# Turning a 128x32 block of row maxima: one TensorE transpose and a copy, or four 32x32 transposes on VectorE

## The chip, the cores and the metric

One core of one Trainium2 chip runs the whole kernel. The metric is the device time of one execution in microseconds. Before the change three runs took 1509.4, 1510.23 and 1512.35 us (median 1510.23).

## The reference

Eight batches of 512 tokens with 128 features go through three blocks: a layer of attention and a mixture of eight experts, an attention layer with rotary positions and shared keys, and the first block again with the same weights. All attention is over the 512 tokens of a batch. Cut to what matters here, it is

```
scores = einsum('bhqd,bhkd->bhqk', q, k) * scale
attn = softmax(scores, axis=-1)
out = einsum('bhqk,bhkd->bhqd', attn, v)
```

with 16 heads of 8 features, and the first and the last block end in

```
one_hot = one_hot(argmax(logits, axis=-1), E)
h = gelu(einsum('td,edh->teh', xf, w1)); y = einsum('teh,ehd->ted', h, w2)
out = einsum('te,ted->td', one_hot, y)
```

The softmax takes away the maximum of each row of scores before its exponential. How the kernel finds that maximum for each query and where it puts it is what the change is about.

## The kernel before

**Stages.** `stream` is the attention program and is built twice: the first with 8 batches (32 passes), the second with 16 batches (64 passes: 8 batches of the middle attention, then 8 of the last block). After and between them the expert blocks run (`experts`). A pass n handles four heads of one batch: 512 queries by 512 keys by 4 heads. It has four steps, kt = 0 to 3.

**Maxima, two passes ahead.** In step kt of pass n, TensorE computes 128 queries x 512 keys of scores for each of the four heads of pass n + 2 (`max_score`, L855), one bank of PSUM each, beside the transposed scores of pass n itself (`score`, L871) and the product of the probabilities with V (`weigh`, L884). VectorE reduces the four banks two at a time (`take_max`, L1251) into two columns of `maxima`. ScalarE takes the exponentials (L1222).

**Splitting.** After step kt = 3 of pass n VectorE has all 16 columns of maxima of pass n + 2: 128 queries on the partitions, a column for each of four heads and four query tiles. `split_max` (L1259, L1261) makes of them a rounded part and the rest, 32 columns of `split`. The second instruction waits for the first.

**Turning and adding.** The maxima go as two more feature rows into Q, so that the matrix product subtracts them. For that they have to lie along the free dimension. `turn_max` on TensorE (L862) transposes the 128x32 block into a bank of the ring, `copy_rows` on VectorE (L1273) copies the 32x128 result to `maxT`, and `rows_of_max` on SyncE (L601) waits for the copy and sends two transfers of 8 KB from `maxT` to Q. `maxT` has two halves used in turn; a half is written anew once the transfers of two passes before have landed (`max_rows`). TensorE waits for `max_rows` at kt = 0 of the pass itself. Behind `rows_of_max(n + 1)` SyncE issues `load(n + 4)`: the zeros, Q and K of four passes ahead.

**The order.** The program on each engine is written out by `Plan`. In pass n it puts, for each kt, the four maxima of pass n + 2 and then a group of other operations that take a bank: at kt = 0 ("rows", n + 1) and what `slot` adds (z, n, a, k, qs, ks: transposes and projections of other batches), at kt = 2 the outputs and others. So VectorE does, from the end of pass n - 1: L1251 twice, `split_max(n + 1)`, L1251 twice (kt = 0 of pass n), `copy_rows(n + 1)`, L1251 twice (kt = 1). TensorE does the step kt = 0, then `turn_max(n + 1)`, the companion, and then the step kt = 1. For n = 0 of each stage both are done at the start of `main`, in a bank outside the ring.

**The ring.** Four banks, used in rotation. An operation takes one bank, but the last of a group of odd size takes two, so that the maxima stay in pairs. TensorE waits, before it fills a bank, until the one who last used it has released it. With "rows" and one companion in a group, the maxima of kt = 1 for the first two heads need the banks that the second L1251 of kt = 0 releases; with "rows" alone it is the same, as "rows" takes two. Of the 94 groups with "rows", 78 have one companion (z in 20, a in 20, k or ks in 20, n in 12, qs in 6). In 16 it is alone: passes 1, 3, 5, 24, 26, 28 and 30 of the first stage, 3, 25, 29, 33, 37, 56, 58, 60 and 62 of the second; their "rows" are those of the pass after.

Of the kernel before, what the change touches and what calls it, by code (L numbers as in the profile page):

```python
# [26 lines left out]
P = 128  # L27
# [23 lines left out]
RING = 4  # L51
# [54 lines left out]
def cols(tile, start, n):  # L106
    return tile[:, bass.ds(start, n)]
# [6 lines left out]
def sems(ctx, nc, tag, names):  # L114

    handles, fields, values = [], [], []
    for entry in names.split():
        name, _, n = entry.partition(":")
        new = [nc.alloc_semaphore(name=f"{tag}_{name}{i}") for i in range(int(n or 1))]
        handles += new  # L120
        fields.append(name)
        values.append(new if n else new[0])

    def clear():
        nc.clear_and_free_semaphores(handles)
        nc.all_engine_barrier()

    ctx.callback(clear)
    return namedtuple("Sems", fields)(*values)
# [141 lines left out]
def load_outputs(eng, c, b):  # L271
# [3 lines left out]


Turn = namedtuple("Turn", "first end engine done")
CONSUMER = {"max": "dve", "rows": "dve", "out": "dve", "gate": "dve", "z": "act", "q": "act", "qs": "act", "k": "act",
            "ks": "act", "v": "act", "a": "act", "proj": "act", "n": "act", "rank": "act"}


class Plan:
# [89 lines left out]

    def group(self, n, kt):
        names = []
        if kt == 0 and 1 <= n + 1 < self.last:
            names += [("rows", n + 1)]
        if kt == 2 and 2 <= n <= self.last and n % 2 == 0:
            names += [("out", n - 1)]
        if kt in (0, 2):
            names += self.slot(n, kt)  # L380
        self.groups[n, kt] = names
        self.put(names)
# [6 lines left out]
def stream(nc, c, ctx, a, label, kinds, past, blocks):  # L389
# [4 lines left out]
    first_ffn = kinds.index(True)  # L394
    gathers = label > 0
    if True:
        s = sems(ctx, nc, f"s{label}", "filled freed evacuated first max_hi split recip max_rows:5 q_loaded:5 k_loaded:5 "
                 "scores probs pv out_copied links dve_links first_stored:2 var_ready std_ready normed renormed stats:2 moments:2 added combined roped hi lo:2 "
                 "stored:2 k_first choices onehot chosen located scattered:2 tabled table tails:2")
        ring, scp = c.bank[0:RING], c.bank[RING:RING + EXPS]  # L400
# [35 lines left out]
        def filled(eng, *name):  # L436
            eng.wait_ge(s.filled, turns[name].end)

        def released(eng, *name):
            t = turns[name]  # L440
            eng.wait_ge(s.freed if t.engine == "dve" else s.evacuated, t.done)
# [124 lines left out]
        def sync(sp):  # L566
# [25 lines left out]
            def rows_of_max(n):  # L592

                g = n % SLOTS
                if n:
                    released(sp, "rows", n)
                else:
                    sp.wait_ge(s.first, 2)
                for tile in range(2):
                    r = TILE * tile + ROWS  # L600
                    sp.dma_start(c.Q[r:r + 2, g * KSLOT:(g + 1) * KSLOT].bitcast(F32).rearrange("i (a n) -> i a n", n=P),  # L601
                                 c.maxT[16 * tile:16 * tile + 16, n % 2 * P:(n % 2 + 1) * P].bitcast(F32))\
                        .then_inc(s.max_rows[g], 16)

            def opening():
                if label == 0:
# [233 lines left out]
        def tensor(pe):  # L840
            def bank_for(*name):
                t = turns[name]
                for u in range(t.first, t.end):
                    if u >= RING:
                        engine, done = plan.release[u - RING]
                        pe.wait_ge(s.freed if engine == "dve" else s.evacuated, done)
                return ring[t.first % RING]

            def fill(ins, *name):
                t = turns[name]  # L850
                ins.then_inc(s.filled, t.end - t.first)
# [3 lines left out]
                fill(nc.tensor.matmul(bank, q4[parts(j), n % SLOTS, j // 2, qt * P:(qt + 1) * P],  # L855
                                      k4[parts(j), n % SLOTS, j // 2, :], start=True, stop=True), "max", n, qt, j)

            def turn_max(n):

                pe.wait_ge(s.split, n + 1)  # L860
                bank = bank_for("rows", n) if n else outp
                ins = nc.tensor.transpose(bank[0:32, 0:P], c.split[:, 32 * (n % 2):32 * (n % 2) + 32].bitcast(F32), c.ident[:, :])  # L862
                if n:
                    fill(ins, "rows", n)
                else:
                    ins.then_inc(s.first, 1)

            def score(n, kt, j):
                x = (n * QT + kt) * J + (j ^ 1)
                wait(pe, s.probs, x - EXPS + 1)  # L870
# [102 lines left out]

            def group(n, kt):
                for kind, i in plan.groups.get((n, kt), ()):
                    if kind == "rows":
                        turn_max(i)
                    elif kind == "rank":
                        rank(i)
                    elif kind == "out":  # L980
                        turn_out(i)
                    elif kind == "z":
                        turn_normed(i)
                    elif kind == "v":
                        project_v(i)
                    elif kind == "a":
                        turn_attended(i)
                    elif kind == "proj":
                        project_out(i)
                    elif kind == "n":  # L990
                        turn_renormed(i)
                    elif kind == "gate":
                        gate(i)
                    else:
                        project(kind, i)
# [50 lines left out]
            def main():  # L1046
                if label:
                    pe.wait_ge(blocks.s.out_copied, HALVES * NBLK)
                turn_max(0)
                loaded(1)  # L1050
                for qt in range(QT):
                    maxima(1, qt)
                for n in range(last):
                    for kt in range(QT):
                        step(n, kt)
                for half in range(2):
                    weigh(last - 1, QT - 1, half)
# [181 lines left out]
        def vector(dve):  # L1239
            def freed(ins, *name):  # L1240
                t = turns[name]
                ins.then_inc(s.freed, t.end - t.first)
# [12 lines left out]
            def split_max(n):  # L1255
# [4 lines left out]
                dve.wait_ge(s.max_hi, n + 1)  # L1260
                nc.vector.tensor_tensor(parts[:, :, 1, :], whole, parts[:, :, 0, :].bitcast(F32), ALU.subtract)\  # L1261
                    .then_inc(s.split, 1)

            def copy_rows(n):
                if n >= 2:
                    dve.wait_ge(s.max_rows[(n - 2) % SLOTS], 32 * ((n - 2) // SLOTS + 1))
                if n:
                    bank = ring[turns["rows", n].first % RING]
                    filled(dve, "rows", n)
                else:  # L1270
                    bank = outp
                    dve.wait_ge(s.first, 1)
                ins = nc.vector.tensor_copy(cols(c.maxT, n % 2 * P, P), bank[0:32, 0:P])  # L1273
                if n:
                    freed(ins, "rows", n)
                else:
                    ins.then_inc(s.first, 1)

            def normalise(n):
                filled(dve, "out", n)  # L1280
# [26 lines left out]

            def group(n, kt):
                for kind, i in plan.groups.get((n, kt), ()):
                    if kind == "rows":  # L1310
                        copy_rows(i)
                    elif kind == "out":
                        normalise(i)
                    elif kind == "gate":
                        add_gate_bias(i)
                        if i >= nb - 2:
                            for step in range(5):
                                choose(i, step)
                            count(nc.vector, link, i)
                        if i == nb - 2:  # L1320
                            locate(nc.vector, link, nb - 3, c.temp[1])
                    elif kind == "rank" and i >= nb - 2:
                        locate(nc.vector, link, i, c.temp[1])
                        if i == nb - 1:
                            table(1)
# [174 lines left out]

            def main():
                split_max(0)
                copy_rows(0)
                all_maxima(1)
                split_max(1)
                for n in range(last):
                    for kt in range(QT):
                        if n + AHEAD < last:
                            take_max(n + AHEAD, kt, 0)
                            take_max(n + AHEAD, kt, 1)  # L1510
                            if kt == QT - 1:
                                split_max(n + AHEAD)
                        group(n, kt)
                        norms(n, kt)
                        choices(n, kt)
                    if n == last - 2:
                        table(0)
                for i in range(2):
                    stored(dve, i, nb)
# [223 lines left out]
def build(nc, a, out):  # L1743
    with ExitStack() as ctx:
        def sb(name, shape, dt=F32):
            return ctx.enter_context(nc.sbuf_tensor(name, shape, dt))
# [25 lines left out]
        c.ident, c.upper, c.ones = sb("ident", [P, P]), sb("upper", [P, P]), sb("ones", [P, P])  # L1772
        c.maxima = sb("maxima", [P, 32])
        c.split = sb("split", [P, 64], F32R)
        c.maxT = sb("maxT", [32, 2 * P], F32R)
        c.warm = sb("warm", [P, 1])
        c.recip = sb("recip", [P, 4 * QT * J])
        c.logits, c.onehot, c.rank = sb("logits", [P, 2 * QT * E]), sb("onehot", [P, 2 * QT * E]), sb("rank", [P, 2 * RANKS])
# [109 lines left out]
```

## Time and profile before

| | |
|---|---|
| median of three runs | 1510.23 us |
| the profiled execution | 1509.52 us, its span 1507.8 us |
| granted TensorE clock, mean | 0.977 of full speed |
| TensorE matmuls | 1377.5 us, 91% of the span, 12036 instructions |
| VectorE | 1176.0 us, 78%, 1898 instructions |
| ScalarE | 1102.9 us, 73% |
| GpSimd | 646.7 us, 43% |
| DMA | 137.57 MB, 91 GB/s |

Busy shares are means over stages. The attention stages are from 45 to 430 us and from 578 to 1365 us; the rest is start, expert blocks and end. Times in the timeline rows count from the start of the span.

### The profile page before, as it was taken

To read this page: it belongs to the slowest core of one execution; us is meant where nothing else is said; L and a number is where in the kernel's file an instruction comes from. 1 tells how busy PE (TensorE), PEld (TensorE's weight loads), DVE (VectorE), ACT (ScalarE), POOL (GpSimd) and SP (SyncE) were. 2 spreads that over 40 slices of the span, in tenths; PEclk is the share of its full clock that TensorE was granted. 3 is DMA by queue.
4 is the path that set the end of the run, shared out by engine and by line. 5 is a ranking of instruction groups with operands and counts; after the bars stand their busy time and mean duration, and the time that the engine had idled before them with its cause. 6 is when DMAs were issued, how large, how long until landed. Compare 5 with 4: busy or idle time off the path is not lost.

```text
span 1507.8 us, 34954 instructions
## 1 busy us (share of the span) xinstructions
PE 1377.5 (91%) x12036; PEld 670.6 (44%) x12036; DVE 1176.0 (78%) x1898; ACT 1102.9 (73%) x2124; POOL 646.7 (43%) x983
## 2 busy tenths in 40 slices
PE   3899999999999997999999999999999999999995
PEld 1333333433338883333333333333333344335995
DVE  6888889888855348888888888888888888894541
ACT  2488877787785563888888888787878777777553
POOL 5224245542226683544364353323334543313753
PEclk8799999999999997999999999999999999999998
DMA  3644433433102425432333243333333333211234
GB/s 90 164 137 117 111 102 98 114 93 86 45 25 60 119 75 160 114 83 69 97 97 83 71 110 86 100 91 79 89 93 84 81 88 100 63 37 37 75 106 120
DMA packets 101485, 137.57 MB, mean 91 GB/s; under 512 B 29792, under 2 KB 72160, under 8 KB 101312
## 3 DMA queue, kind: packets, MB, share of 16 engines
q1 hardware_dynamic: 70768, 85.69, 19.9%
q0 software_dynamic: 24256, 45.31, 12.3%
q10 hardware_dynamic: 6288, 4.34, 1.0%
q8 instruction: 100, 1.64, 0.5%
q14 instruction: 73, 0.60, 0.1%
HBM read 79.05 MB, written 53.51 MB: 88 GB/s over the span
## 4 chain that ended last, share of the span: by engine, by line
PE 58%; DVE 28%; issue 7%; DMA 3%; POOL 2%; ACT 1%; SPq 0%; DVEq 0%; POOLq 0%; ACTq 0%
DVE maxima L1251 25%; PE banks L884 16%; PE banks L871 12%; PE banks L855 11%; PE banks L1610 4%; PE banks L912 4%; PE banks L1619 4%; PE banks L894 2%; PE banks L938 2%; PE banks L919 1%; DMA by_token<-work 1%; PE banks L954 1%; DVE split L1259 1%; DVE stats L1329 1%; DMA work<-sorted_x 1%
## 5 line engine op out<-in xcount | busy, mean ns | idle before, releaser
L1251 DVE TENSOR_REDUCE maxima<-banks 128x2 f32<-128x1024 f32 x768 | 924.1, 1222 | 154.9 <-PE banks L855 146.8
L1222 ACT ACTIVATE work<-banks 128x512 f32<-128x512 f32 x1536 | 829.6, 598 | 155.5 <-PE banks L871 140.6
L855 PE MATMUL banks<-K,Q 64*128 64x512 f32 x1536 | 568.2, 459 | 46.5 <-DVE maxima L1251 36.4
L871 PE MATMUL banks<-Q,K 64*128 64x512 f32 x1536 | 566.2, 450 | 0.5
L884 PE MATMUL banks<-work,V 128*18 128x256 f32 x6144 | 481.6, 386 | 1.5 <-ACT work L1222 0.8
L855 PEld LDWEIGHTS banks<-K,Q 64*128 64x128 f32 x1536 | 228.2, 189 | 200.8 <-DVE maxima L1251 135.4
L871 PEld LDWEIGHTS banks<-Q,K 64*128 64x128 f32 x1536 | 228.9, 185 | 177.4 <-ACT work L1222 128.3
L884 PEld LDWEIGHTS banks<-work,V 128*18 128x18 f32 x6144 | 103.3, 96 | 275.1 <-issue 199.8
L723 POOL TENSOR_TENSOR lo<-full,hi 128x512 fp32r<-128x512 f32 x40 | 51.1, 1278 | 245.6 <-ACT hi L1097 144.1
L1619 PE MATMUL banks<-w,work 128*128 x736 | 99.6, 279 | 0.6 <-ACT work L1653 0.6
L1673 DVE COPY work<-w 128x512 f32 x88 | 43.9, 499 | 71.8 <-PE banks L1610 58.6
L1593 POOL DMA_INDIRECT by_token<-work x76 | 76.0, 1000 | 45.7 <-ACT work L1653 34.4
L1610 PE MATMUL banks<-work 128*128 128x128 f32 x704 | 93.8, 276 | 0.7 <-DVE work L1673 0.7
L1619 PEld LDWEIGHTS banks<-w,work 128*128 128x128 f32 x736 | 91.1, 195 | 1.7 <-issue 1.5
L1610 PEld LDWEIGHTS banks<-work 128*128 128x128 f32 x704 | 86.0, 192 | 3.6 <-issue 2.1
L1648 ACT ACTIVATE work<-banks 128x512 f32<-128x512 f32 x92 | 54.8, 596 | 32.6 <-PE banks L1610 32.4
L139 POOL TENSOR_SCALAR root<-moments 128x4 f32<-128x4 f32 x38 | 8.9, 235 | 157.7 <-DVE moments L1336 156.9
L704 POOL DMA_INDIRECT sorted_x<-N,pos x64 | 65.2, 1018 | 19.9 <-issue 11.6
L1643 ACT ACTIVATE work<-banks,ln 128x128 f32<-128x128 f32 x92 | 41.9, 455 | 24.2 <-PE banks L1603 17.2
L545 POOL TENSOR_TENSOR full<-full,cos_sb 128x512 f32<-128x512 f32 x12 | 15.4, 1288 | 102.2 <-ACT swap L1091 102.1
L140 POOL TENSOR_TENSOR rstd<-root,minus_half 128x4 f32<-128x4 f32 x52 | 54.4, 1047 | 4.4
L1095 ACT ACTIVATE full<-banks 128x512 f32<-128x512 f32 x44 | 26.3, 598 | 40.5 <-PE banks L912 34.8
(193 smaller groups left out, 1268.4 us busy)
## 6 DMA issues: line engine op xcount, KB each, us to landing
Q<-q_scratch SPq DMA_DIRECT2D x188, 128.0 KB, 2.6
K<-k_scratch SPq DMA_DIRECT2D x376, 64.0 KB, 2.5
Q<-zero_rows SPq DMA_DIRECT2D x182, 64.0 KB, 2.2
q_scratch<-hi POOLq DMA_DIRECT2D x40, 256.0 KB, 4.7
q_scratch<-lo POOLq DMA_DIRECT2D x40, 256.0 KB, 6.8
k_scratch<-hi POOLq DMA_DIRECT2D x20, 256.0 KB, 4.5
k_scratch<-lo POOLq DMA_DIRECT2D x20, 256.0 KB, 6.3
work<-sorted_x SPq DMA_DIRECT2D x76, 66.0 KB, 2.0
```

The source lines that it names most:

```text
L140: link(eng.tensor_tensor(out, half, c.minus_half[:, :], ALU.pow))
L704: nc.gpsimd.indirect_dma_start(c.sorted_x[:, :], bass.IndirectOffsetOnAxis(ap=c.pos[:, t:t + 1], axis=0), c.rows[:, t, :], None).then_inc( ...
L855: fill(nc.tensor.matmul(bank, q4[parts(j), n % SLOTS, j // 2, qt * P:(qt + 1) * P], k4[parts(j), n % SLOTS, j // 2, :], start=True, stop=T ...
L871: nc.tensor.matmul(scp[x % EXPS][:, :], k4[parts(j), n % SLOTS, j // 2, kt * P:(kt + 1) * P], q4[parts(j), n % SLOTS, j // 2, :], start=Tr ...
L884: ins = nc.tensor.matmul(outp[32 * j:32 * j + 2 * V1, q], v4[:, n // G % VSLOTS, kt, n % G // 2, j, V1 * odd:V1 * odd + 2 * V1], prob[:, k ...
L912: fill(nc.tensor.matmul(bank, w[:, i * D:(i + 1) * D], c.zT[:, :], start=True, stop=True), kind, b)
L1222: nc.scalar.activation(prob[:, kt, j ^ 1, :], scp[x % EXPS][:, :], ACT.Exp, scale=SCALE).then_inc(s.probs, 1)
L1251: nc.vector.tensor_reduce(c.maxima[:, at:at + 9:8], c.banks[:, k * S:(k + 2) * S].rearrange("p (m n) -> p m n", m=2), AX.X, ALU.max).then_ ...
L1593: nc.gpsimd.indirect_dma_start(c.by_token[:, :], bass.IndirectOffsetOnAxis(ap=x_sb(i)[:, D:D + 1].bitcast(U32), axis=0), y_sb[i % ring], N ...
L1610: ins = nc.tensor.matmul(hp[i % 2][:, t * P:(t + 1) * P], w1(i)[:, t * P:(t + 1) * P], uT[i % 2], start=True, stop=True)
L1619: ins = nc.tensor.matmul(yp, h[i % 2][:, t * P:(t + 1) * P], cols(c.w2, at + t * D, D), start=(t == 0), stop=(t == HT - 1))
L1648: nc.scalar.activation(h[i % 2], hp[i % 2][:, :], ACT.Gelu_apprx_tanh).then_inc(s.gelu, 1)
```

## The change

The transpose of the maxima leaves TensorE and the copy leaves VectorE; VectorE turns the block itself in four 32x32 transposes, 32 queries each, straight behind the split, and writes the results side by side to the 32 partitions of `maxT`. A wait for the split's second instruction stands ahead of them, and the wait for the older transfers moves there too. SyncE waits for the semaphore `max_turned`. "rows" is no longer in the plan, so it takes no bank. The two transfers are the same. `maxT` is a plain float32 tile.

```diff
-CONSUMER = {"max": "dve", "rows": "dve", "out": "dve", ...
+CONSUMER = {"max": "dve", "out": "dve", ...
     def group(self, n, kt):
         names = []
-        if kt == 0 and 1 <= n + 1 < self.last:
-            names += [("rows", n + 1)]
...
             def rows_of_max(n):
                 g = n % SLOTS
-                if n:
-                    released(sp, "rows", n)
-                else:
-                    sp.wait_ge(s.first, 2)
+                sp.wait_ge(s.max_turned, n + 1)
...
-            def turn_max(n):
-                pe.wait_ge(s.split, n + 1)
-                bank = bank_for("rows", n) if n else outp
-                ins = nc.tensor.transpose(bank[0:32, 0:P], c.split[:, 32 * (n % 2):32 * (n % 2) + 32].bitcast(F32), c.ident[:, :])
...
             def main():
...
-                turn_max(0)
                 loaded(1)
...
             def split_max(n):
...
                 nc.vector.tensor_tensor(parts[:, :, 1, :], whole, parts[:, :, 0, :].bitcast(F32), ALU.subtract)\
                     .then_inc(s.split, 1)
-
-            def copy_rows(n):
                 if n >= 2:
                     dve.wait_ge(s.max_rows[(n - 2) % SLOTS], 32 * ((n - 2) // SLOTS + 1))
-                if n:
-                    bank = ring[turns["rows", n].first % RING]
-                    filled(dve, "rows", n)
-                else:
-                    bank = outp
-                    dve.wait_ge(s.first, 1)
-                ins = nc.vector.tensor_copy(cols(c.maxT, n % 2 * P, P), bank[0:32, 0:P])
...
+                dve.wait_ge(s.split, n + 1)
+                for t in range(4):
+                    at = n % 2 * P + 32 * t
+                    ins = nc.vector.transpose(c.maxT[:, at:at + 32], c.split[32 * t:32 * t + 32, 32 * (n % 2):32 * (n % 2) + 32].bitcast(F32))
+                ins.then_inc(s.max_turned, 1)
...
             def main():
                 split_max(0)
-                copy_rows(0)
                 all_maxima(1)
...
-        c.maxT = sb("maxT", [32, 2 * P], F32R)
+        c.maxT = sb("maxT", [32, 2 * P])
```

## Rows read from the trace of the kernel before

**Rows 1.** Part 4 of the page: shares of the chain that ended last, by engine.

```profile
PE 58%; DVE 28%; issue 7%; DMA 3%; POOL 2%; ACT 1%; SPq 0%; DVEq 0%; POOLq 0%; ACTq 0%
```

**Rows 2.** Windows: length; busy (count) of PE, PEld, DVE, ACT, POOL; clock, DMA, GB/s.

```profile
44.53:430.00 385.47, 362.12 (x3236) 147.38 (x3234) 338.67 (x504) 297.43 (x555) 140.72 (x261) 0.98 0.38 101
589.00:1362.40 773.40, 737.62 (x6636) 295.27 (x6633) 673.85 (x961) 623.27 (x1167) 308.06 (x470) 1.00 0.33 87
```

**Rows 3.** What L855 waited for, whole span: us and times.

```profile
  DVE maxima L1251: 171.8, 319
```

**Rows 4.** Chain in order of time: start, us, what; first and last L1259.

```profile
42.83 0.18 DVE split L1259
...
1349.94 0.19 DVE split L1259
```

**Rows 5.** Timeline of VectorE, pass with z: start, us, instruction, idle before.

```profile
1135.07 0.17 DVE L1259 CAST split<-maxima 128x16 fp32r<-128x16 f32 x1
1135.27 0.17 DVE L1261 TENSOR_TENSOR split<-maxima,split 128x16 fp32r<-128x16 f32 x1
1135.37 2.35 DVE L1251 TENSOR_REDUCE maxima<-banks 128x2 f32<-128x1024 f32 x2
1137.63 0.27 DVE L1273 CAST maxT<-banks 32x128 fp32r<-32x128 f32 x1
...
1138.61 2.48 DVE L1251 TENSOR_REDUCE maxima<-banks 128x2 f32<-128x1024 f32 x2 [0.31 <-PE banks L855]
...
1141.52 0.38 DVE L1336 BATCH_NORM_AGGREGATE moments<-stats 128x2 f32<-128x6 f32 x4
```

**Rows 6.** Timeline of TensorE, the same pass.

```profile
1136.73 0.27 PE L862 MATMUL banks<-ident,split 128*32 128x128 f32 x1
...
1137.77 0.49 PE L855 MATMUL banks<-K,Q 64*128 64x512 f32 x1 [0.29 <-DVE maxima L1251]
```

**Rows 7.** Timeline, VectorE and TensorE, a pass with k.

```profile
910.84 2.35 DVE L1251 TENSOR_REDUCE maxima<-banks 128x2 f32<-128x1024 f32 x2
...
912.20 0.27 PE L862 MATMUL banks<-ident,split 128*32 128x128 f32 x1
...
912.32 1.10 PE L912 MATMUL banks<-zT,wqk 128*128 128x512 f32 x2
...
913.35 0.49 PE L855 MATMUL banks<-K,Q 64*128 64x512 f32 x1
```

**Rows 8.** Groups by line: busy us, mean ns of one, idle before.

```profile
L862 PE MATMUL banks<-ident,split 128*32 128x128 f32 x96 | 26.3, 274 | 29.8 <-DVE maxima L1251 20.2 <-DVE split L1261 4.2 <-issue 1.7
L1273 DVE CAST maxT<-banks 32x128 fp32r<-32x128 f32 x96 | 25.9, 269 | 3.4 <-PE banks L862 3.4
...
L1336 DVE BATCH_NORM_AGGREGATE moments<-stats 128x2 f32<-128x6 f32 x160 | 15.2, 157 | 1.4
```

**Rows 9.** Timeline, VectorE and TensorE, a pass with "rows" alone.

```profile
899.90 2.35 DVE L1251 TENSOR_REDUCE maxima<-banks 128x2 f32<-128x1024 f32 x2
...
902.30 0.50 PE L855 MATMUL banks<-K,Q 64*128 64x512 f32 x1 [0.66 <-DVE maxima L1251]
...
903.14 2.48 DVE L1251 TENSOR_REDUCE maxima<-banks 128x2 f32<-128x1024 f32 x2 [0.71 <-PE banks L855]
```

**Rows 10.** Timeline of TensorE, a pass with a.

```profile
1175.96 0.27 PE L862 MATMUL banks<-ident,split 128*32 128x128 f32 x1 [0.85 <-DVE maxima L1251]
...
1177.01 0.50 PE L855 MATMUL banks<-K,Q 64*128 64x512 f32 x1 [0.29 <-DVE maxima L1251]
```

**Rows 11.** Timeline of VectorE at the start of the first stage.

```profile
43.04 0.18 DVE L1261 TENSOR_TENSOR split<-maxima,split 128x16 fp32r<-128x16 f32 x1
...
43.71 0.28 DVE L1273 CAST maxT<-banks 32x128 fp32r<-32x128 f32 x1 [0.49 <-PE banks L862]
...
44.53 9.14 DVE L1251 TENSOR_REDUCE maxima<-banks 128x2 f32<-128x1024 f32 x8 [0.55 <-PE banks L855]
```

**Rows 12.** Waits of SyncE's own queue: us, times, longest.

```profile
SPq L601 <- DVE maxT L1273: 618.1, 94, 11.2
```

## What is forecast, and from what

> **What bounds the kernel now.** I read the views from coarse to fine. The shares of the chain that ended last [rows 1]: TensorE 58%, VectorE 28%, and nearly all of VectorE's part is the row maxima, L1251. So the two alternate; neither is the bound alone. The windows over the two attention stages [rows 2] say how close they are: in 773.4 us TensorE is busy 737.6 and VectorE 673.9. Only there does the edit act: 31 passes in the first, 63 in the second, and one pass at the start of each.
>
> What ties them is the ring of four banks. TensorE fills two banks, VectorE reduces them in one L1251, and TensorE may not go on before the banks are free: it sat idle 171.8 us, 319 times, in front of L855 until an L1251 had ended [rows 3]. A step costs VectorE two L1251 (2.48 us back to back, [rows 5]) and TensorE nearly as much, so each engine's extra work shows up as waiting of the other.
>
> Then the place of the edit. The chain in order of time goes through the first split instruction (L1259) in 75 of its 96 executions; the first and the last are in [rows 4]. In the timeline of an ordinary pass boundary [rows 5]: split 1135.07 and 1135.27, L1251 twice from 1135.37 to 1137.72, only then copy_rows at 1137.63, next L1251 at 1138.61 after 0.31 us of waiting for TensorE's fill. TensorE's side [rows 6]: L862 at 1136.73, z's transposes behind it, and L855 at 1137.77 after 0.29 us of waiting for the second L1251. So what stands between the split and those two L1251 is paid in full, and what comes behind them (copy_rows) lies in VectorE's idle time.
>
> The 21 splits that are off the chain have hardly any slack: in the pass of [rows 7] L862 starts 912.20 with no wait shown, but the first L1251 of the pair ended about 912.08 (910.84 plus 1.24) and the second 913.19; L855 came at 913.35. I count them like the others.
>
> **The change, part by part.**
>
> *The four transposes, in VectorE between split and L1251.* Today the pair goes L1259, wait, L1261 and, without a wait, L1251 0.10 us after L1261 began [rows 5]. After: L1261, a wait for it, four transposes, L1251. The wait makes the first transpose start 0.21 us after L1261, the distance at which L1261 follows L1259, for which it waits in the same way (42.83 to 43.04, [rows 4, 11]). Then three more starts at a distance s; the last one hands on to L1251 as L1261 did. So the path grows by X = 0.21 + 3s.
>
> For s there is no row of a transpose on VectorE. Below: small instructions with no wait between them overlap; the four L1336 take 0.38 us together [rows 5] at 157 ns each [rows 8], a distance of (0.38 - 0.157)/3 = 0.075; for L1261 (0.17) followed by L1251 it was 0.10. Above: the 32-partition copy from PSUM, 269 ns [rows 8], s = 0.28. Between them: 0.21, a small instruction (0.17, L1259 and L1261) that must have ended before the next begins. A transpose has 32 elements where L1259 has 16, reads and writes SBUF like it, and three of the four turn to another 32 partitions than their forerunner; I take the row without overlap, s = 0.21, X = 0.84. It is the largest choice in this forecast. Ends: X = 0.44 and 1.05.
>
> The Trainium skill (VectorE: DVE Perf Modes, "Two Vector instructions with no wait between them") has a rule that speaks against this change: an instruction whose input starts in another group of 32 partitions than the last one's is held until every earlier one has finished. By the overlapping L1336 of [rows 5] the sum below would be +30 to +35 us, by this rule about +61; no row here has an input on another group, so the trace can't say. The same page's table of transpose paths gives 311 ns for VectorE's over 128 columns; if each of the four cost that, X would be 1.14 and the sum +88, an estimate from that page.
>
> *Which passes pay.* 94 of the 96 turns sit in a group at kt = 0. In 78 of them another operation shares the group (20 z, 20 a, 20 k or ks, 12 n, 6 qs). "rows" took one bank and its companion one; alone the companion takes two. So the ring is as before, L855 of the next step still needs the second L1251, and these pay X: 78 x 0.84 = +65.5.
>
> In the other 16 "rows" stood alone and its two banks vanish. There L855 needs only the first L1251. At [rows 9]: L1251 pair from 899.90, L855 at 902.30 after 0.66 us of wait, next L1251 at 903.14 after 0.71 us of idle. After: first L1251 ends 899.90 + 0.84 + 1.24 = 901.98, L855 at about 902.02, its maxima are filled 0.84 later at 902.86, but VectorE ends the second L1251 only at 902.25 + 0.84 = 903.09. It goes on at 903.1 as before. 14 passes x 0. The last two of the 16 (k = 31 and 63) have no L1251 left to delay; they lose L862's 0.27: -0.5.
>
> *L862 removed from TensorE.* 274 ns each [rows 8]. With a short companion (z, a, n: 52 passes) it already lies in front of a wait for the second L1251 ([rows 6]; in [rows 10], where statistics come before the maxima, it waits 0.85 and L855 another 0.29): nothing. With k, ks or qs (26 passes) TensorE's queue is longer by one 1.10 us pair L912; in [rows 7] L855 came 913.35 and the second L1251 had ended 913.19, with 0.04 to be handed on: 0.12 comes back, 26 x 0.12 = -3.1.
>
> *copy_rows removed from VectorE.* 25.9 us [rows 8], all in front of idle time: 0.31 in [rows 5], 0.71 in [rows 9]. It would be worth 0.2 to 0.27 a pass only if VectorE had no idle left there; after the edit TensorE is the later one at that point as before, since both are pushed by X. Nothing.
>
> *The start of each stage.* Today VectorE waits for L862 (0.49) and for the first fill behind it (0.55): split 42.83, L1251 at 44.53, 1.70 us [rows 4, 11]. After: 0.21 + 0.21 + 4 x 0.21 = about 1.15, and TensorE fills meanwhile. -0.55, twice: -1.1.
>
> *The moved waits.* VectorE's wait for max_rows of two passes before now stands behind the split; those transfers were issued a whole pass (about 12 us) earlier and TensorE needs them before its own scores, so it is met. If not, everything on VectorE would stand behind it. SP waits for VectorE's word instead of copy_rows', about 1.6 us earlier (today the copy ends 1137.90, 2.83 after L1259; then 0.21 + 0.84 + 0.19); it spent 618.1 us waiting there [rows 12]. Its two transfers of 8 KB and the loads queued behind them start earlier, for slots needed one and more passes later. Nothing for the time. Longer waits of TensorE could lower its clock; at waits of 0.85 and 0.29 in one pass [rows 10] the granted clock was 1.00 of full speed (2.4 GHz) over the second stage [rows 2], so I leave that out.
>
> **Sum**: 65.5 - 3.1 - 1.1 - 0.5 = +60.8 us. The profiled execution took 1509.52 us (span 1507.8), the median shown is 1510.23, 0.7 apart. 1510.2 + 60.8 = 1571 us, 4% slower.
>
> **Rivals.**
> 1. *The transposes overlap* like the L1336. s = 0.10: X = 0.51, 78 x 0.51 - 4.7 = +35, 1545 us; s = 0.075: 1540. For: every unwaited pair of small instructions in the trace does so. Against: all those stay on the same partitions.
> 2. *The transposes are dearer*, s = 0.28: X = 1.05, 81.9 - 4.7, and 0.2 in each of the 14 passes where VectorE then is late: +80, 1590. For: copy_rows, which writes the same tile, takes 269 ns. Against: 32 elements is few.
> 3. *The other side: TensorE is the bound and VectorE has room.* 100 us of VectorE idle in the second stage [rows 2] would take in the 0.84, and 94 x 0.27 of L862 would be saved: 1510 - 25 = 1485. It decides where the second L1251 ends before TensorE's group does, with over 0.84 to spare. For: TensorE is busy 95%. Against: [rows 6, 9, 10] show TensorE waiting for exactly that L1251, and 75 of 96 splits are on the chain.
> 4. *It doesn't save what it says and costs nothing either*: X as hidden as copy_rows is. That needs the idle time to lie ahead of the pair, and it lies behind it. 1510.
>
> **Chances.** Forecast 0.60, rival 1 0.23, rival 2 0.08, rival 3 0.06, rival 4 0.03. Over 0.2% (3 us, about what this kernel's runs can tell from no change) slower in the forecast and rivals 1 and 2: 0.91; faster 0.06; same 0.03. The range takes in the bounds of s from 0.075 to 0.28: 1538 to 1592.
>
> **What would show it.** In the changed profile: the transposes' distance (0.21 for right, 0.10 for rival 1); from L1259 to the first L1251 of the pair 1.15 us instead of 0.30; L855 of the next step waiting for L1251 as often as now or oftener; VectorE's idle for L855 unchanged at some 0.6 to 0.85 in the shared passes; a mean pass of the second stage near 12.9 us, where 773.4 / 63 is 12.3 now; SP's transfers out before the first L1251 ends. Wrong would be: a pair of L1251 after the transposes whose end TensorE doesn't wait for, or transposes on idle time.

## The result and the profile after

The changed kernel takes 1609.8 us (median of four runs, 1604.0 to 1612.5) beside 1511.3 for the kernel before: ratio 1.065 [1.061, 1.068]. The forecast was 1571 with a range of 1538 to 1592: the right side, but the change is 98.5 us where 60.8 were forecast, 38 too little. In the changed file VectorE's maxima are L1232, the split L1240 and L1242, the transposes L1249, TensorE's L849 and L855 are the score products, L896 and L912 the companions k (or ks, qs) and a.

The profiled execution took 1607.25 us, 97.7 more than that of before. The page's shares of the chain, by engine and by line, answer to [rows 1]:

```profile
PE 48%; DVE 38%; issue 6%; DMA 3%; POOL 2%; SPq 1%; ACT 1%; DVEq 0%; POOLq 0%; ACTq 0%
DVE maxima L1232 29%; PE banks L868 12%; PE banks L855 10%; PE banks L849 9%; DVE maxT L1249 4%; PE banks L896 4%; PE banks L1580 3%; PE banks L1589 3%; PE banks L878 2%; PE banks L922 1%; PE banks L903 1%; POOL by_token L1563 1%; DVE split L1240 1%; DVE stats L1300 1%; DVE split L1242 1%
```

VectorE's part rose from 28 to 38%, and L1249, the new line, holds 4% of the chain, some 64 us of 1605. What L849 waited for, answering to [rows 3] (171.8 us, 319 times before):

```profile
  DVE maxima L1232: 208.1, 314
```

The four transposes and their neighbours, in a pass with z on VectorE (answers to [rows 5]):

```profile
1214.71 0.17 DVE L1240 CAST split<-maxima 128x16 fp32r<-128x16 f32 x1
1214.92 0.18 DVE L1242 TENSOR_TENSOR split<-maxima,split 128x16 fp32r<-128x16 f32 x1
1215.20 0.84 DVE L1249 STREAM_TRANSPOSE maxT<-split 32x32 f32<-32x32 f32 x4
1215.97 2.30 DVE L1232 TENSOR_REDUCE maxima<-banks 128x2 f32<-128x1024 f32 x2
1218.31 0.49 DVE L1300 BATCH_NORM_STATS2 stats<-Y 128x6 f32<-128x128 f32 x2
1219.17 2.48 DVE L1232 TENSOR_REDUCE maxima<-banks 128x2 f32<-128x1024 f32 x2 [0.38 <-PE banks L849]
```

The first L1232 starts 1.26 us after L1240 where it was 0.30, so 0.96 later; the pair is 0.05 shorter (2.30 against 2.35; the trace doesn't say why). Net 0.91. The idle time for TensorE's fill, 0.38 where it was 0.31, is still there, so what was removed behind the pair gave nothing.

Then a pass with a on TensorE (answers to [rows 10]), and after it the windows over a stretch behind that wait and one behind the same wait in another pass:

```profile
982.52 0.63 PE L912 MATMUL banks<-ident,N 128*128 128x128 f32 x4 [1.88 <-DVE maxima L1232]
983.61 0.79 PE L849 MATMUL banks<-K,Q 64*128 64x512 f32 x1 [0.45 <-DVE maxima L1232]
...
987.89 0.79 PE L849 MATMUL banks<-K,Q 64*128 64x512 f32 x1
```

```profile
core 0: us, PE busy (x) PEld busy (x) DVE busy (x) ACT busy (x) POOL busy (x), PEclk, DMA share, GB/s
983.00:991.00 8.00, 7.55 (x50) 2.41 (x48) 4.37 (x5) 4.34 (x8) 6.20 (x15) 0.57 0.28 76
820.00:828.00 8.00, 7.35 (x68) 3.50 (x72) 6.09 (x6) 5.53 (x11) 5.87 (x11) 1.00 0.55 151
```

In both passes TensorE had waited 1.88 us, done 0.63 us of transposes and waited another 0.45 or 0.46. Behind the first the granted clock is 0.57 over 8 us (most of it at the lower level, 1.2 GHz) and L849 takes 0.79 instead of 0.49; behind the second it stays 1.00. In the kernel before the longest wait of TensorE in the attention stages, their starts left out, was 0.97 us, and its clock did not fall there. That is the part which the forecast left out.

I took the distance from each first split instruction to the next one in both profiled executions and sorted the differences by the companion in the group. Up to rounding the sum is the whole change up to the last split:

| passes | number | longer by, us | each |
|---|---|---|---|
| k, ks | 20 | +19.4 | 0.97 |
| z, without the first pass of each stage | 18 | +16.7 | 0.93 |
| n and qs | 18 | +16.4 | 0.91 |
| first pass with a ring place, k = 1 | 2 | +3.1 | |
| a, granted clock 1.00 in the 9 us from the start of L912 | 8 | +7.8 | 0.98 |
| a, granted clock 0.62 (six) or 0.81 to 0.82 (six) there | 12 | +37.3 | 3.11 |
| alone | 14 | +0.2 | |
| starts, and the stretch between the stages | | -3.4 | |
| all | | +97.5 | |

All twelve passes with a and over 1.5 us of difference have a lower clock in that stretch, and none of the eight others has. Sixteen of the 20 wait 1.88 us, and all twelve are among them; the other four, where no statistics stand ahead of the maxima, wait 0.94. In two of the twelve the clock fell just at the start of the transposes (0.1 us ahead of it, or with it), and there is no second wait: it is not needed for the fall.

### The profile page after: what moved, and what is told of

Read it like the earlier page. It is cut to its first block, busy times and chain, and to the rows that moved or that the text cites. A ratio compares the mean times of both kernels' runs of the same rounds, so it can differ in the third digit from the quotient of the medians.

```text
span 1605.5 us, 34980 instructions
## 1 busy us (share of the span) xinstructions
PE 1389.6 (87%) x11940; PEld 669.1 (42%) x11940; DVE 1235.2 (77%) x2186; ACT 1101.6 (69%) x2124; POOL 645.0 (40%) x983
## 4 chain that ended last, share of the span: by engine, by line
PE 48%; DVE 38%; issue 6%; DMA 3%; POOL 2%; SPq 1%; ACT 1%; DVEq 0%; POOLq 0%; ACTq 0%
DVE maxima L1232 29%; PE banks L868 12%; PE banks L855 10%; PE banks L849 9%; DVE maxT L1249 4%; PE banks L896 4%; PE banks L1580 3%; PE banks L1589 3%; PE banks L878 2%; PE banks L922 1%; PE banks L903 1%; POOL by_token L1563 1%; DVE split L1240 1%; DVE stats L1300 1%; DVE split L1242 1%
## 5 line engine op out<-in xcount | busy, mean ns | idle before, releaser
L1232 DVE TENSOR_REDUCE maxima<-banks 128x2 f32<-128x1024 f32 x768 | 919.2, 1216 | 180.3 <-PE banks L849 173.7
L849 PE MATMUL banks<-K,Q 64*128 64x512 f32 x1536 | 582.6, 469 | 63.3 <-DVE maxima L1232 53.3
L855 PE MATMUL banks<-Q,K 64*128 64x512 f32 x1536 | 580.1, 460 | 0.2
L868 PE MATMUL banks<-work,V 128*18 128x256 f32 x6144 | 493.6, 394 | 2.0 <-ACT outT L1057 1.1
L849 PEld LDWEIGHTS banks<-K,Q 64*128 64x128 f32 x1536 | 234.7, 193 | 227.4 <-DVE maxima L1232 154.8
L855 PEld LDWEIGHTS banks<-Q,K 64*128 64x128 f32 x1536 | 234.7, 190 | 185.0 <-ACT work L1203 137.0
L1249 DVE STREAM_TRANSPOSE maxT<-split 32x32 f32<-32x32 f32 x384 | 76.9, 200 | 14.4 <-DVE split L1242 0.9
```

The source lines that it names most:

```text
L855: nc.tensor.matmul(scp[x % EXPS][:, :], k4[parts(j), n % SLOTS, j // 2, kt * P:(kt + 1) * P], q4[parts(j), n % SLOTS, j // 2, :], start=Tr ...
L868: ins = nc.tensor.matmul(outp[32 * j:32 * j + 2 * V1, q], v4[:, n // G % VSLOTS, kt, n % G // 2, j, V1 * odd:V1 * odd + 2 * V1], prob[:, k ...
L1232: nc.vector.tensor_reduce(c.maxima[:, at:at + 9:8], c.banks[:, k * S:(k + 2) * S].rearrange("p (m n) -> p m n", m=2), AX.X, ALU.max).then_ ...
L1249: ins = nc.vector.transpose(c.maxT[:, at:at + 32], c.split[32 * t:32 * t + 32, 32 * (n % 2):32 * (n % 2) + 32].bitcast(F32))
```

## The experiments

Runs of one group shared their runs of the kernel before. Medians and ratios to it are given; "per pass" is the difference from split to split as above.

**1. The statistics moved away from the pair (changed kernel).**

```diff
                         group(n, kt)
-                        norms(n, kt)
+                        if n % G == 3 and kt == 0:
+                            norms(n - 1, QT - 1)
+                        if not (n % G == 2 and kt == QT - 1):
+                            norms(n, kt)
```

> The changed kernel with one thing moved: the statistics that stand between the four transposes and the next row maxima (third and fourth tile and the moments, 0.87 us, in 18 passes, nearly all with companion a) now stand behind those maxima. Clock theory: in those passes TensorE waits 1.88 and 0.45 us and its granted clock falls to half for 4 to 7 us afterwards, some 27 us in all; with the wait about 0.8 shorter the clock stays up, so this saves the statistics' own 10 us or so and the 27: about 1573 us, mean granted clock back near 0.975. Rival (the passes with a are long for another reason, VectorE's queue or a companion's bank): it saves as much as the same move saves in the kernel before, about 10: 1599, clock as in the changed kernel.

1573.5 us (1571.9 to 1575.0), ratio 1.042 [1.039, 1.045], mean granted clock 0.971 against 0.958. TensorE in a pass with a:

```profile
965.12 0.63 PE L912 MATMUL banks<-ident,N 128*128 128x128 f32 x4 [0.94 <-DVE maxima L1232]
966.21 0.49 PE L849 MATMUL banks<-K,Q 64*128 64x512 f32 x1 [0.46 <-DVE maxima L1232]
```

The wait is 0.94 shorter and L849 keeps its 0.49. All 20 passes with a have a granted clock of 1.00 and none is over 0.92 longer than before: 6.1 us in all, where they were 45.1. But the statistics now lengthen waits in the passes with z, and in four of those the clock fell, behind waits of 1.18 to 1.42 us. One of them, and the window over it:

```profile
1188.44 0.63 PE L885 MATMUL banks<-ident,normed 128*128 128x128 f32 x4 [1.42 <-DVE maxima L1232]
1189.53 0.50 PE L849 MATMUL banks<-K,Q 64*128 64x512 f32 x1 [0.46 <-DVE maxima L1232]
```

```profile
core 0: us, PE busy (x) PEld busy (x) DVE busy (x) ACT busy (x) POOL busy (x), PEclk, DMA share, GB/s
1188.40:1197.40 9.00, 8.50 (x60) 3.15 (x60) 7.43 (x15) 5.12 (x9) 2.18 (x7) 0.81 0.28 77
```

In eight other passes with z, waits of 1.30 to 1.77 us left the clock at 1.00. So 1.88 us is not the length from which it starts.

**2. The same move in the kernel before.** The same edit.

> The kernel before with the same move of the statistics. Both theories: they leave the path between the split and the maxima (0.78 us in each of 18 passes) and fall behind it into 0.6 us of idle time, so 18 x 0.55 = 10 us are saved: 1500, clock unchanged at 0.977, as it did not fall in these passes before.

1501.8 us (1499.4 to 1504.6), ratio 0.994 [0.992, 0.996]. So the move itself is worth 8 us, and 36 in the changed kernel: the other 28 are what the clock accounts for, its four new falls taken off. Sixteen passes with a became 0.78 shorter, 12 of the passes with z behind them 0.3 to 0.5 longer; the reason for the latter was not tested.

**3 and 4. Transposes behind the pair in the passes with a only, or with z only.** The turn becomes a function of its own, called where the copy stood when the pass has that companion. For a:

```diff
+            def early_turn(n):
+                return not any(kind == "a" for kind, _ in plan.groups.get((n - 1, 0), ()))
...
                                 split_max(n + AHEAD)
+                                if early_turn(n + AHEAD):
+                                    turn_rows(n + AHEAD)
+                        if kt == 0 and n + 1 < last and not early_turn(n + 1):
+                            turn_rows(n + 1)
                         group(n, kt)
```

> The changed kernel, but in the 20 passes whose companion is a the four transposes stand behind the next step's row maxima, where the copy stood. Clock theory: saves 20 x 0.9 on the path, some 27 us of slow clock, and loses up to 5 as VectorE's idle time there (0.6 to 0.9) is shorter than 1.1: about 1567 to 1572. Rival (each pass pays the same 0.9 and the rest has another cause): 1593 to 1597.

> The same as the one before it for the 20 passes whose companion is z instead of a. Both theories: these passes keep their clock, so only the path counts, 20 x 0.9 = 18, less what no longer fits in VectorE's idle time there (0.3 plus 0.27 of the copy against 1.1, 20 x 0.5): 1590 to 1600. The difference between this run and the a run is what sets the a passes apart; rival theory says none over 5 us.

With a: 1562.6 us (1561.6 to 1564.1), ratio 1.035 [1.032, 1.038]; the passes with a are +0.2 us in all, where they were +45.1. With z: 1578.4 us, but from 1571.6 to 1585.0, ratio 1.047 [1.043, 1.051]; the passes with z are +1.8 where they were +16.7. In its profiled execution (1571.55 us) the clock fell in only 4 of the passes with a instead of 12, though TensorE waits there as long as in the changed kernel, and in the two passes k = 4, which have no companion, behind waits of 2.02 and 1.83 us that the changed kernel has too and kept its clock behind. So the a run saved 47 us, a little beyond the clock theory's 38 to 43 and far from the rival's 13 to 17; the z run saved 31 where 10 to 20 were expected, the rest again clock, this time in passes that the edit did not touch. The four runs' width is part of the same thing: they took 1571.6, 1575.5, 1581.4 and 1585.0 us at mean granted clocks of 0.972, 0.966, 0.962 and 0.959. How often the clock falls differs from one kernel and one execution to the next.

**10 and 11. The converse: transposes early in the passes with a only, or z only,** on the late version (6, below). `early_turn` is then true for the passes with that companion alone.

> The late version (1502 us) with the four transposes back at the early place in the 20 passes whose companion is a, and only there. Clock theory: 20 x 1.0 on the path and 1.5 or 2.8 more in those of them in which the granted clock falls after the long wait, 6 to 12 of 20: 1502 + 20 + 10 to 30 = 1532 to 1552, mean granted clock 0.96 to 0.97. Rival (no clock cost, each pass pays the same): 1522, clock as in the late version, 0.976.

> The late version with the transposes back at the early place only in the 20 passes whose companion is z. Both theories: 20 x 0.9 less the 0.13 to 0.27 that the late place costs in some of these passes, clock unmoved: 1502 + 16 = 1518.

With a: 1542.4 us (1541.6 to 1546.3), ratio 1.021 [1.019, 1.023], clock 0.961. With z: 1520.0 (1518.2 to 1522.0), 1.006 [1.004, 1.008], clock 0.974 to 0.977. Both came out as expected. Twenty passes with the same four instructions at the same place cost 41 us over the late version's 1501.8 or 18. With a the clock fell in 11 passes (33.5 us of difference in them, 9.1 in the nine others); with z in none. TensorE's wait with a is that of the changed kernel, here in a pass that kept its clock:

```profile
997.87 0.63 PE L912 MATMUL banks<-ident,N 128*128 128x128 f32 x4 [1.88 <-DVE maxima L1232]
998.95 0.50 PE L849 MATMUL banks<-K,Q 64*128 64x512 f32 x1 [0.46 <-DVE maxima L1232]
```

**5. All four transposes from the same 32 partitions.**

```diff
-                    ins = nc.vector.transpose(c.maxT[:, at:at + 32], c.split[32 * t:32 * t + 32, 32 * (n % 2):32 * (n % 2) + 32].bitcast(F32))
+                    ins = nc.vector.transpose(c.maxT[:, at:at + 32], c.split[0:32, 32 * (n % 2):32 * (n % 2) + 32].bitcast(F32))
```

> The changed kernel, but all four transposes read the first 32 partitions of the split (so three quarters of the turned maxima are those of other queries; everything else is left as it is). Theory: in the changed kernel they start 0.21 us apart at 0.20 each, one after the other, because each begins on another group of 32 partitions; on one group they should overlap and start about 0.12 apart, 0.27 less in each of 78 passes, 21 us, and a little more where the clock no longer falls: 1575 to 1588. Rival (a transpose never overlaps its neighbour): distance 0.21, time as in the changed kernel, 1610.

1558.9 us (1552.6 to 1562.5), ratio 1.032 [1.028, 1.035], 51 less than the changed kernel. VectorE:

```profile
1186.94 0.17 DVE L1240 CAST split<-maxima 128x16 fp32r<-128x16 f32 x1
1187.15 0.18 DVE L1242 TENSOR_TENSOR split<-maxima,split 128x16 fp32r<-128x16 f32 x1
1187.43 0.48 DVE L1249 STREAM_TRANSPOSE maxT<-split 32x32 f32<-32x32 f32 x4
1187.85 2.30 DVE L1232 TENSOR_REDUCE maxima<-banks 128x2 f32<-128x1024 f32 x2
```

Four take 0.48 instead of 0.84. The first takes 0.200 in both kernels; the other three 0.157 here, 0.136, 0.093 and 0.093 after the one before, and 0.200 in the changed kernel, 0.213 after it. On one group they overlap, on changing groups each begins when the one before is done. The passes with k, ks, n and qs are on average 0.52 to 0.55 longer than before instead of 0.89 to 1.01. The result is 16 to 29 us below what I expected: some 30 us over 78 passes came from the path (0.36 to 0.5 a pass and not 0.27), 6 from the passes alone, and 12 from the clock. It still fell in 9 of the 16 passes with a that have statistics, behind waits of 1.36 us (one 1.60), with 0.81 over the 9 us in each; in the changed kernel six had 0.62.

**6. The four transposes behind the pair in every pass.**

```diff
+            def early_turn(n):
+                return False
```

> The changed kernel with the four transposes in every pass behind the next step's two row maxima, where the copy stood. Place theory: cost is a matter of place, 1.1 us of VectorE there lies in the 0.6 to 0.9 us (with the copy's own 0.27) of its idle time, the path is as before, and TensorE is rid of its transpose: 1504 to 1510. Rival (VectorE's total load counts: 0.57 more in 94 passes, up to 53): 1530 or more.

1501.8 us (1498.6 to 1506.0), ratio 0.993 [0.992, 0.995]: 108 us less than the changed kernel with the same instructions, 2 below the range expected, and 10 less than the kernel before. The window over the second stage:

```profile
core 0: us, PE busy (x) PEld busy (x) DVE busy (x) ACT busy (x) POOL busy (x), PEclk, DMA share, GB/s
589.00:1362.00 773.00, 731.66 (x6582) 290.32 (x6580) 705.24 (x1153) 622.52 (x1170) 307.62 (x469) 1.00 0.32 87
```

VectorE is busy 31 us more than in [rows 2] and the stage is no longer: from its first to its last split it takes 783.1 us, where it took 784.5. The shared passes with a, k, ks, n and qs differ from before by -0.10 to 0.19, those with z by -0.36 to 0.44, 1.4 us in all. The one clear gain between splits is in the passes where "rows" stood alone, -4.3 us over 14, with the pair not delayed; that it comes from the two banks, or from L862 being gone, was not tested apart. The profiled execution was the slowest of the four, 3.5 us shorter than that of before; where the rest of the 10 us between the medians lies isn't shown.

**7. One transpose over 128 partitions, eight transfers, early.**

```diff
-                for t in range(4):
-                    at = n % 2 * P + 32 * t
-                    ins = nc.vector.transpose(c.maxT[:, at:at + 32], c.split[32 * t:32 * t + 32, ...
-                ins.then_inc(s.max_turned, 1)
+                at = 32 * (n % 2)
+                nc.vector.transpose(c.maxT[:, at:at + 32], c.split[:, at:at + 32].bitcast(F32)).then_inc(s.max_turned, 1)
...
+                    for t in range(4):
+                        at = 32 * t + 16 * tile
+                        sp.dma_start(c.Q[r:r + 2, ...].rearrange("i (a n) -> i a n", n=P)[:, :, 32 * t:32 * t + 32],
+                                     c.maxT[at:at + 16, 32 * (n % 2):32 * (n % 2) + 32]).then_inc(s.max_rows[g], 16)
```

> The changed kernel with one transpose instruction over 128 partitions and 32 columns at the same early place instead of four, its four blocks left on their own partitions and carried on in eight transfers of 2 KB instead of two of 8. Theory: three distances of 0.213 leave the path, X falls from 0.91 to about 0.27, TensorE's longest wait to about 1.25 and its clock stays up: 78 x 0.27 - 5 = +16, 1524 to 1530. Rival (the six more transfers take SyncE's queue, 0.6 us each, and come late for something): above 1540.

The counts that the waits for these transfers ask for, and the shape of `maxT`, follow. 1541.9 us (1536.7 to 1545.9), ratio 1.019 [1.017, 1.022]. The path did as the theory said, about 0.3 in nearly every shared pass that kept its clock (one transpose of 0.21). But the rival is right too:

```profile
61.31 0.79 PE L852 MATMUL banks<-K,Q 64*128 64x512 f32 x1 [10.19 <-DMA Q<-maxT]
```

```profile
1181.82 0.21 DVE L1251 STREAM_TRANSPOSE maxT<-split 128x32 f32<-128x32 f32 x1
1181.95 2.33 DVE L1235 TENSOR_REDUCE maxima<-banks 128x2 f32<-128x1024 f32 x2
```

At 61.31 TensorE has waited 10.19 us for the turned rows. SyncE issued the eight transfers of pass 0 from 44.22 to 49.50, 0.61 to 0.67 us each, but their packets, of 128 bytes where they were of 512, ran on until 60.8, beside the five loads of X issued right behind them. In the second stage TensorE waited 10.79 us in the same place, with sixteen such transfers issued from 593.2 to 608.1. How much of this is the issues and how much the packets was not tested apart. The two passes k = 1 are 21.2 us longer than before. That TensorE's "clock stays up" was wrong as well: it fell in 5 of the passes with a, behind waits of only 1.10 us, 8.8 us of difference in them, and in five others with the same 1.10 it did not.

```profile
1209.98 0.63 PE L915 MATMUL banks<-ident,N 128*128 128x128 f32 x4 [1.10 <-DVE maxima L1235]
1211.06 0.69 PE L852 MATMUL banks<-K,Q 64*128 64x512 f32 x1 [0.46 <-DVE maxima L1235]
```

```profile
core 0: us, PE busy (x) PEld busy (x) DVE busy (x) ACT busy (x) POOL busy (x), PEclk, DMA share, GB/s
1210.00:1218.00 8.00, 7.54 (x57) 3.05 (x58) 5.82 (x7) 4.94 (x9) 6.70 (x17) 0.79 0.26 77
```

**8. The same late, with the statistics moved.** Experiment 7's instruction and transfers in 6's place with 1's edit.

> One transpose and eight transfers, placed behind the next step's row maxima, and the statistics moved behind them as well: a candidate for the fastest. Theory: nothing of it on the path, TensorE's transpose gone (3 us in the passes with k, ks or qs), 8.5 us from the statistics as in the kernel before with that move: 1495 to 1500. Rival (the transfers' issues late): 1505 or more.

1532.1 us (1526.1 to 1535.4), ratio 1.014 [1.011, 1.017]: my theory is wrong by 35 us and the rival right. Waits for the transfers, us in all, times and longest:

```profile
PEld banks L852 <- DMA Q<-maxT: 51.4, 19, 11.3
PE banks L852 <- DMA Q<-maxT: 42.3, 14, 10.7
```

In experiment 7 the second line read 28.1, 12 and 10.8. That the later place leaves SyncE too little time for its eight issues fits this, and was not tested by itself. The clock (0.963) fell in seven passes behind waits of 1.6 to 3.4 us for these transfers.

**9. The four late, with the statistics moved.** Experiment 6 with 1's edit.

> Four transposes behind the next step's row maxima in every pass, two transfers, and the statistics moved behind those maxima too: the candidate for the fastest. Place theory: the two gains add, 8.5 us from the statistics (as they gave in the kernel before) and 8 to 10 from the transposes' move (as measured against the kernel before), unless both want the same idle time in the passes with a, 0.9 us of it against 1.95: then the sum is 5 to 10 us instead of 17. Range 1493 to 1504. Rival (the gains don't share a place): 1493 at once.

1505.4 us (1503.7 to 1508.6), ratio 0.996 [0.995, 0.998]: 1 us above the range, and no better than either edit alone (1501.8 each, from other groups of runs). The sixteen passes with a and statistics are 0.23 to 0.44 shorter, where the move alone gave 0.78. Ten of the passes with z behind them are 0.5 to 1.0 longer and an eleventh 2.1, its clock fallen behind a wait of 1.14 us. That the two moves ask for the same idle time, as one half of the expectation said, fits this.

## Why the forecast was wrong

**The bound and the place: right.** What stands between split and pair is paid in full (+0.91 to +0.97 in 56 shared passes; 6 shows that behind the pair it is free), also in the 16 passes with k, ks or qs whose split was off the chain: +0.84 to +0.96, and one of +1.43.

**X: undersized by 0.12.** The forecast was 0.21 + 3 x 0.21 = 0.84. Measured: L1242 to the first transpose 0.28 (not 0.21), three distances of 0.213 (as forecast), last transpose to L1232 0.14, where L1261 to L1251 was 0.09; 0.96, less 0.05 from the shortened pair. Over 78 passes 0.07 net is 5 us.

The choice of s was right. The rule of the Trainium skill (VectorE: DVE Perf Modes, "Two Vector instructions with no wait between them"), that an instruction on another group of 32 partitions is held until the earlier ones have finished, agrees with the runs: 0.213 between changing groups, 0.108 on average on the same one (experiment 5). The transposes of the changed kernel also read one group and write another, which experiment 5 removed too. But the trace of the changed kernel has instructions that do not: where L1300 is the first to read SBUF after the transposes, as at 1218.31 above, it starts 0.03 us after L1232 has ended, in all 12 cases; in the 12 others, as in the kernel before, it starts 0.09 before that end. Rival 1 fell with it, and so did the dearer estimate of X = 1.14: the four transposes took 0.84 together.

**L862 removed, -3.1 forecast: nothing came.** The passes with k are among the longest (1.01 on average), those with ks and qs (0.89 and 0.90) near those with n (0.91). The prediction read [rows 7] as if TensorE had not waited for the first L1251 because no wait is shown in front of L862. It had: its pair L912 started 0.27 us after that L1251's end, and L862 stood in this time. Without L862 the pair, now L896, starts 0.26 after it:

```profile
845.53 2.30 DVE L1232 TENSOR_REDUCE maxima<-banks 128x2 f32<-128x1024 f32 x2
...
846.96 1.10 PE L896 MATMUL banks<-zT,wqk_rot 128*128 128x512 f32 x2 [1.10 <-DVE maxima L1232]
...
847.98 0.50 PE L849 MATMUL banks<-K,Q 64*128 64x512 f32 x1
```

From L896 to L849 it is 1.03 us, as from L912 to L855 before. L849 starts 0.15 after the second L1232's end, and 0.055 where it waits for that end, so it is this pair of matmuls that comes last.

**copy_rows, the moved waits, alone passes, starts: right but for small sums.** +0.2 over 14 alone passes against 0; -0.6 for the starts against -1.1 (the prediction's own terms for the start add up to 1.26 us, not 1.15); SyncE waited more (729 us against 618), and in one pass TensorE waited 1.56 us for its transfers.

**The step that failed: "Longer waits of TensorE could lower its clock; at waits of 0.85 and 0.29 in one pass the granted clock was 1.00 ..., so I leave that out."** The row was right and the step past it wrong: X falls on top of 0.85 in exactly these passes, so by the prediction's own terms the wait to ask about was 0.85 + 0.84 = 1.69 us (1.88 measured), and no row of before shows the clock kept over such a wait. The falls cost 12 x (3.11 - 0.98) = 26 us in the profiled execution. Experiments 1, 3 and 10 show it from three sides: shorten the wait by another instruction, move the transposes in these passes, bring them back. With 26 added, and 5 for X and 3 for L862, the forecast's 61 is 95 of the measured 98. The range had no term for the clock either; it reached to 1592 by dearer transposes alone.

**What stays open.** Why the clock falls behind 12 of 16 waits of 1.88 us and not behind the other four, or behind 4 of 16 in experiment 4; the waits, what precedes them and what follows look alike in the timeline. The length of the wait alone doesn't decide it: in experiment 7 the clock fell behind 1.10 us in five passes and was kept behind 1.39 in another. And in the passes with k, ks and qs of the changed kernel, which wait 1.09 to 1.56 us, it never fell. Where the wait was 1.88 us (the changed kernel, experiments 4 and 10), each fall began between 0.2 us ahead of the start of the transposes and 2.2 us behind it. What the runs do show is that the falls are tied to the longer waits: in all thirteen profiles no fall inside the attention stages, their starts left out, stands behind waits of less than 1.10 us. To keep TensorE busy during the wait was not tried.

## What to carry to other kernels

When two engines take turns, ask of an added instruction whether it stands before or behind the operation that the other engine waits for; with the same four the kernel took 98 us more than before when they stood ahead of it, and 10 less when they stood behind it. Sum the new wait with the one that the pass has already, and where the sum goes beyond any wait of TensorE that the trace shows at full clock, the clock is a cost of its own and belongs in the range. Small VectorE instructions that each read another group of 32 partitions did not overlap here; one over all four groups took as long as one of them, but its result lay so that eight small transfers took the place of two, and TensorE waited over 10 us for them at the start of each stage.

## What the runs showed of the hardware

- Idle times of TensorE of 1.88 us, with 0.63 us of transposes behind them and mostly a second one of up to 0.46, came with a granted clock of 1.2 GHz for some of the next 9 us in 12 of 16 passes (11 of 16 in experiment 10, 4 of 16 in 4). With 1.36 to 1.60 in the first place it was 9 of 16 (experiment 5), with 1.10 5 of 10 (7), with 0.94 none of 20 (1). A pass of the changed kernel in which it fell lost 1.0 to 2.9 us over one in which it did not.
- A 32x32 transpose of float32 on VectorE took 0.200 us, and 0.213 to the next when the group of partitions changed. Behind one of the same group it took 0.157, and the distance was 0.093 to 0.136. One over 128 partitions and 32 columns took 0.21.
- A transpose that waits for the instruction before it started 0.28 us after that one's start, where L1261 behind L1259 needed 0.21.
